# Recurrent layers: token mixes in pairs of row groups, token additions one item later

## The reference, cut to what matters

```
xa = _ln(x, ln1_w, ln1_b)
sx = jnp.concatenate([state[:, 1:2] - xa[:, :1], xa[:, :-1] - xa[:, 1:]], axis=1)
xxx = jnp.tanh((xa + sx * maa_x) @ maa_w1).reshape(b, l, 5, DM)
xxx = jnp.einsum('blfd,fde->blfe', xxx, maa_w2)
xm = xa[:, :, None] + sx[:, :, None] * (maa_stack + xxx)
xk, xw, xv, xr, xg = (xm[:, :, j] for j in range(5))
w = jnp.exp(-jnp.exp(time_decay + jnp.tanh(xw @ td_w1) @ td_w2)).reshape(b, l, h, s_)
r = (xr @ Wr.T).reshape(b, l, h, s_)
k = (xk @ Wk.T).reshape(b, l, h, s_)
v = (xv @ Wv.T).reshape(b, l, h, s_)
g = jax.nn.silu(xg @ Wg.T)
# the scan over the tokens: out = r (u * k v + s), s = k v + w * s
```

## Time and profile before

| what | value |
|---|---|
| median of 3 runs | 3045.12 us (3043.93 to 3047.5) |
| the profiled execution | 3048.42 us, its span 3046.6 us |
| mean granted clock of TensorE | 0.961 of full speed |
| TensorE (PE) busy | 2794.7 us, 92% |
| VectorE (DVE) busy | 2018.4 us, 66% |
| ScalarE (ACT) busy | 1340.0 us, 44% |
| GpSimd (POOL) busy | 665.8 us, 22% |
| one turn of the loop in L1 | 78.40 us |

### The profile page before, as it was taken

One profiled execution on the slowest core, in us unless ns is written; L12 is line 12 of the kernel. 1 busy time (PEld: TensorE's weight loads), 2 busy tenths in 40 slices (PEclk: granted clock), 3 DMA queues, 4 the chain that ended last, 5 costly groups with the idle time before them and its releaser, 6 DMA issues.

```text
span 3046.6 us, 53530 instructions
## 1 busy us (share of the span) xinstructions
PE 2794.7 (92%) x18016; PEld 2172.7 (71%) x18016; DVE 2018.4 (66%) x4920; ACT 1340.0 (44%) x3438; POOL 665.8 (22%) x436
## 2 busy tenths in 40 slices
PE   7999999878999999589999999999997889999986
PEld 7555555766888888485445554899996768888866
DVE  2778787668999999554555555411101799999992
ACT  1888888533444443353444444323220234444432
POOL 0011110034444445200000000000000444444440
PEclk9999999988999999889999999999997999999998
DMA  2101000323332333200000000300002333333340
GB/s 108 37 24 35 24 34 13 131 77 93 93 93 87 92 87 96 80 28 20 21 20 29 19 19 10 153 1 1 0 0 90 104 93 91 91 88 90 92 125 11
DMA packets 96168, 182.86 MB, mean 60 GB/s; under 512 B 10122, under 2 KB 87498, under 8 KB 92462
## 3 DMA queue, kind: packets, MB, share of 16 engines
q1 hardware_dynamic: 96046, 181.27, 19.2%
HBM read 171.34 MB, written 9.90 MB: 59 GB/s over the span
## 4 chain that ended last, share of the span: by engine, by line
PE 67%; DVE 13%; issue 10%; ACT 8%; POOL 1%; DMA 1%; DVEq 0%; SPq 0%; ACTq 0%; POOLq 0%
PE psum L519 20%; PE psum L314 10%; PE psum L1964 6%; PE psum L1851 4%; PE psum L1337 3%; DVE psum L726 3%; PE psum L510 3%; ACT arena L1617 3%; ACT arena L2231 2%; PE psum L1864 2%; PE psum L1906 2%; PE psum L526 2%; PE psum L1349 2%; DVE arena L741 2%; PE psum L533 2%
## 5 line engine op out<-in xcount | busy, mean ns | idle before, releaser
L519 PE MATMUL psum<-arena 128*128 128x200 f32 x4096 | 774.4, 348 | 51.2 <-DVE arena L902 18.6
L519 PEld LDWEIGHTS psum<-arena 128*128 128x128 f32 x4096 | 724.1, 198 | 135.7 <-issue 79.9
L1140 POOL TENSOR_TENSOR arena<-arena 128x800 f32<-128x800 f32 x256 | 454.9, 1780 | 453.8 <-DVE psum L726 453.8
L741 DVE TENSOR_TENSOR_SCAN arena<-arena,psum 128x808 f32<-128x808 f32 x256 | 469.9, 1835 | 37.2 <-PE psum L510 22.0
L314 PE MATMUL psum<-arena 128*128 128x200 f32 (+1 forms) x1920 | 332.4, 335 | 15.1 <-POOLq L139 13.4
L314 PEld LDWEIGHTS psum<-arena 128*128 128x128 f32 x1920 | 328.4, 192 | 16.9 <-POOLq L139 13.3
L1617 ACT ACTIVATE arena<-arena 100x361 f32<-100x361 f32 x512 | 300.4, 590 | 87.2 <-DVE arena L1545 85.5
L1120 POOL TENSOR_TENSOR arena<-arena 128x800 f32<-128x800 f32 x80 | 141.3, 1767 | 775.3 <-DVE arena L749 600.2
L726 DVE TENSOR_TENSOR psum<-arena 128x808 f32<-128x808 f32 x256 | 280.3, 1095 | 6.6 <-DVE arena L741 1.7
L1545 DVE CUSTOM_DVE_ANT_0 arena<-psum,arena 100x361 f32<-100x361 f32 x512 | 254.0, 530 | 45.5 <-ACT arena L1617 37.9
L1337 PEld LDWEIGHTS psum<-arena 100*128 100x128 f32 x1536 | 146.3, 142 | 131.1 <-ACT arena L1629 60.3
(11 more groups left out here) (142 smaller groups left out, 3855.1 us busy)
## 6 DMA issues: line engine op xcount, KB each, us to landing
arena<-v_rows SPq DMA_DIRECT2D x512, 202.0 KB, 3.2
arena<-ctxT SPq DMA_DIRECT2D x32, 722.0 KB, 4.3
arena<-L_w SPq DMA_DIRECT2D x9, 1024.0 KB, 10.1
arena<-L_w SPq DMA_DIRECT2D x8, 1152.0 KB, 16.0
v_rows<-arena SPq DMA_DIRECT2D x32, 202.0 KB, 2.1
arena<-L_fc SPq DMA_DIRECT2D x4, 1024.0 KB, 8.0
arena<-L_pj SPq DMA_DIRECT2D x4, 1024.0 KB, 15.8
arena<-xT SPq DMA_DIRECT2D x4, 800.0 KB, 12.2
```

What stands on the lines that cost most here:

```text
L519: mm = pe.matmul(chunk(bank, j), m.W[n][:, k, c * P:(c + 1) * P], src[:, k, :], start=k == 0, stop=k == C - 1)
L741: dve.tensor_tensor_scan(m.ring[n % 4].rearrange("p j e -> p (j e)"), m.we[:, cc].rearrange("p j e -> p (j e)"), m.kv, 0.0, ALU.mult, ALU. ...
L1140: pool.tensor_tensor(sv, sv, rb, ALU.mult).then_inc(sem("r_states"), 1)
```

## The change

The change does four things.

1. Mixes 0 and 1 become one pair, 2 and 3 another. `mix(x)` now makes two chunks of both members of its pair, x even chunks 0 and 1, x odd chunks 2 and 3. The matmuls alternate between the two members: each member has its own 32 rows of the array and its own bank (4 or 5). Mix 4 stays as it was (`last_mix`).
2. `mix_term(x)` follows: it writes two chunks of each member. xm[0] is complete only after half of mix term 1, xm[1] after the whole of it, xm[2] and xm[3] likewise in mix term 3.
3. The token additions stand at items 9 to 13 instead of 8 to 11 and 13. The place before the item's product, and behind its wait for VectorE's next product, is the same.
4. TensorE does mix 2 and the variance ahead of the k projection, and mix 3 directly behind it, ahead of the decay's first matmul.

Some waits of VectorE move with the data that they guard.

```
             def mix(x):
-                w, th, r0 = (m.w2, m.tha, DM * x) if x < 4 else (m.low, m.thl, BACK)
+                for j in range(2):
+                    for n in range(2):
+                        r0, c = DM * (x - x % 2 + n), 2 * (x % 2) + j
+                        mm = pe.matmul(chunk(4 + n, j), m.w2[r0:r0 + DM, c * P:(c + 1) * P], m.tha[r0:r0 + DM, :],
+                                       start=True, stop=True)
+                mm.then_inc(sem("mix_sum"), 1)
+
+            def last_mix():
                 for c in range(C):
-                    mm = pe.matmul(chunk(4 + c // 2, c % 2), w[r0:r0 + DM, c * P:(c + 1) * P], th[r0:r0 + DM, :],
-                                   start=True, stop=True)
+                    mm = pe.matmul(chunk(4 + c // 2, c % 2), m.low[BACK:BACK + DM, c * P:(c + 1) * P],
+                                   m.thl[BACK:BACK + DM, :], start=True, stop=True)
                 mm.then_inc(sem("mix_sum"), 1)
...
             if front:
+                wait(pe, "mix_term", f, 8)
+                mix(2)
+            if back:
+                m.n2.pe_var(pe, b)
+            if front:
                 wait(pe, "mixed", f, 1)
                 if rec and not back:
                     wait(pe, "gate", i, 2)
                 project_half("k", m.xm[0], 0, 2, "k_sum")
-                wait(pe, "mix_term", f, 8)
-                mix(2)
-            if back:
-                m.n2.pe_var(pe, b)
+                wait(pe, "mix_term", f, 12)
+                mix(3)
...
                 mm.then_inc(sem("decay_hidden_sum"), 1)
-
-                wait(pe, "mix_term", f, 12)
-                mix(3)
                 wait(pe, "mixed", f, 3)
...
                 wait(pe, "decay_rate", f, 4)
-                mix(4)
+                last_mix()
...
             def mix_term(x):
                 wait(dve, "mix_sum", f, x + 1)
-                for c in range(C):
-                    dve.scalar_tensor_tensor(m.xm[x][:, c, :], chunk(4 + c // 2, c % 2), vec(f"stack{x}", c),
-                                             m.sx[:, c, :], ALU.add, ALU.mult).then_inc(sem("mix_term"), 1)
+                for n in range(2):
+                    for j in range(2):
+                        c, y = (2 * (x % 2) + j, x - x % 2 + n) if x < 4 else (2 * n + j, x)
+                        dve.scalar_tensor_tensor(m.xm[y][:, c, :], chunk(4 + n, j), vec(f"stack{y}", c),
+                                                 m.sx[:, c, :], ALU.add, ALU.mult).then_inc(sem("mix_term"), 1)
...
             def add_token(x):
-                wait(pool, "mix_term", f, 4 * x + 4)
+                wait(pool, "mix_term", f, (6, 8, 14, 16, 20)[x])
                 pool.tensor_tensor(seq(m.xm[x]), seq(m.xm[x]), m.xs[:, :, :, 1:E], ALU.add).then_inc(sem("mixed"), 1)
...
-                if front and 8 <= n < 12:
-                    add_token(n - 8)
-                if front and n == 13:
-                    add_token(4)
+                if front and 9 <= n < 14:
+                    add_token(n - 9)
```

More of the change, by code:

```diff
@@ L852, in body @@
                     wait(dve, "k_sum", i, 2)
+                    wait(dve, "decay", i, 4)
                 mix_term(0)
@@ L865, in body @@
             if front:
-                if rec:
-                    wait(dve, "decay", i, 4)
                 mix_term(1)
@@ L874, in body @@
                     wait(dve, "v_sum", i, 2)
+                    wait(dve, "r_sum", i, 2)
+                if not rec and after.tail:
+                    dve.wait_ge(*after.done)
+                    columns()
                 mix_term(2)
@@ L884, in body @@
             if front:
[L885 to L889, removed]
                 mix_term(3)
```

## The result

The changed kernel takes 3273.28 us (median, 3271.07 to 3275.72), the kernel before 3045.49 us beside it. The ratio is 1.0739 with a 95% interval of 1.0725 to 1.0752. The change makes the kernel 7.4% slower; the forecast was 3266 us, or 7.2%.

A forecast was written before the change was run, and what follows sets the result against it. TensorE and VectorE both nearly full, the turn hanging on product 11, addition 2, v, `reduce(4)`, scan 12. 11.7 us waits plus 5.3 clock, 17 a turn: 12 x 17 + 2 x 8.6 = 221 us, forecast 3266, range 3160 to 3325.

The forecast's parts named there:

- The place that decides: Loop turn: addition 2 follows product 12, v starts at 29.5 instead of 21.95; r at 40.56 instead of 28.89.
- the clock terms of the prediction: Half clock behind new pauses, per turn: k 0.8, v 2.1, `reduce(4)` 0.2, r 2.0, mix 4 0.2; 5.3 us.
- a wait of 2.7 us ahead of the scaling: VectorE's scaling behind scan 11 could start at 21.1, but ScalarE's reciprocal deviation, made after k, is ready at 23.8.
- the walk: Predicted timeline of one loop turn, offsets from its first o projection; 11.7 us longer at full clock.
- 8.6 stood for each in the sum: First recurrent call per layer, without second norm: about 6 us of waits and 2.6 for the clock; 2 x 8.6 = 17.
- Both clock rivals: TensorE's clock stays full (3198 us, chance 0.22), or everything behind a pause is at half clock (3330, chance 0.17).
- Full clock: Rival: TensorE's clock stays full, only waits count; 152 us more, 3198 us; chance 0.22.
- Half clock for everything: Rival: everything behind a TensorE pause at half clock, 9.9 us a turn instead of 5.3; 3330 us; chance 0.17.
- The rule of strict order in start and end: Skill's rule for TensorE matmuls: five pass times left of eight in a pair, a mix saves 0.51 us, not 0.67.
- The rival that pairs don't run side by side: Mix 2 ends 0.67 us later, variance and k pushed 0.5 to 1 us a turn; about 3276 us; chance 0.08.
- The rival that the kernel gains the mixes' time: TensorE is the bound: 0.67 us saved 4 times in each of 16 fronts, 43 us, 3002 us; chance 0.03.

The follow-up runs named there:

- the filling run: Changed kernel plus matmuls that nobody reads in TensorE's three pauses, only where rec and back are there, wait for k moved ahead of the filling: 3197.88 us.
- the run with both repairs: Changed kernel with token additions ahead of GpSimd's wait for VectorE's next product, and ScalarE making the reciprocal deviation before moving k out of PSUM: 3145.19 us.
- the run that makes it true: Changed kernel with both members of a pair taken from the same 32 rows: 3304.33 us, ratio 1.0848.

## Why the prediction was right

**The place that decides.** The step that put v behind product 12, and r behind product 13, was right in kind and in size. Offsets from the start of the turn, forecast at full clock and measured with the half clock in it: mix 2 13.95 and 13.24, k 16.8 and 16.49, v 29.5 and 29.95, r 40.56 and 43.38, the feed-forward projection 45.8 and 51.26. With the clock terms of the prediction added (0.8 up to v, 3.1 up to r, 5.3 in all) the last three are 30.3, 43.7 and 51.1. In the filling run, which is at full clock, mix 2, k, v, r and the feed-forward projection start at 13.25, 16.07, 28.80, 39.71 and 44.97, all 0.7 to 0.9 us before the forecast for full clock (13.95, 16.8, 29.5, 40.56 and 45.8): one early error, and every step behind it right to 0.2 us. The run with only the additions moved shows that their place alone is enough.

**ScalarE.** Forecast was a wait of 2.7 us ahead of the scaling, measured 3.76. VectorE reached it 0.7 us earlier than in the walk (at 20.4 instead of 21.1), since a copy of 8 columns took 0.17 us instead of the 0.99 that it took before; this is the early error. Exp was done 0.4 us later than forecast, in part because k, at a lower clock, ended late (at 20.05 instead of 19.8). At full clock, in the filling run, the wait is 2.68 us. Turning the order around gave back 43 us.

**Waits and clock.** A turn was forecast at 11.7 us of waits and 5.3 of clock. By the filling run they are 10.8 and 6.3. That the sum of 17.0 holds (measured 17.1) is partly luck, since two errors cancel: the walk's waits were 0.9 too long, and the clock was taken 1.0 too low. The terms of the clock were all off by a little. The variance and k took 1.5 us more than at full clock where 0.8 stood (the variance 2.38 instead of 1.55, k 3.56 instead of 2.90, start to next start), v 2.5 where 2.1 stood and r 2.6 where 2.0 stood, while `reduce(4)` and mix 4 lost nothing where 0.2 each stood (0.81 and 1.54 us to the next start). Not all of this delays what follows, so the sum is the 6.3 of the filling run.

The first call with recurrence became 6.8 us longer in L1 and 10.9 in L3, where 8.6 stood for each in the sum. The 221 us of the whole sum are 222.7 between the two profiled executions; that the medians are 228 apart comes from which executions were profiled, 2.9 us above the median of its kernel before and 2.2 below it after.

Both clock rivals are settled. Full clock was forecast at 3198, which is what the filling run takes (3197.88), though a hit this close is chance: the run has no filling in the first calls, and its waits are 0.9 us a turn shorter than the rival's. Half clock for everything was forecast at 3330, and `reduce(4)` and mix 4, as short as at full clock, show that it doesn't hold. The Trainium skill (TensorE: Matmul & The Clock Gate, HAM oscillation) describes a kernel whose waits between bursts of matmuls are long enough that each burst begins throttled. v and r in the changed kernel agree with it (granted clock 0.52 and 0.51 behind 7.46 and 5.58 us). It doesn't follow that every new pause is paid for: v behind 3.32 us in the run with both repairs took 2.97 us.

**The pairs.** 0.88 us for a mix was forecast from rows of another layer and measured to the hundredth. The rule of strict order in start and end (the Trainium skill, TensorE: Matmul & The Clock Gate, Part 3), weighed against it, would have given 1.05 us, and 1.38 for the members one after the other. The trace disagrees with it for these matmuls: 0.88 us in both runs. The rival that pairs don't run side by side was priced at about 10 us; the run that makes it true costs 31, because mix 2 and what stands behind it fell into half clock.

**The side.** The rival that the kernel gains the mixes' time had its condition right: the third addition would have had to be done by 21.8 us of the turn, it was done at about 29.8.

## What to carry to other kernels

Where two engines are both nearly full in a loop, shortening work on one is worth nothing in front of a wait; look first which result gates the next long stretch, and follow its place through the order of every engine. When a piece moves on one engine, read the order of the engines that serve it too: here ScalarE still took k before the variance. A wait that opens can cost twice on TensorE, once as a pause and once as half clock on what follows; whether it does has to be looked up in every turn and not in one.

## What the runs showed of the hardware

- Four K=32 matmuls from two row groups into two banks took 0.88 us in both orders that were tried, 1.54 us from one row group. Eight passes in about the time of four.
- 12.6 us a turn of products that nobody reads, put into the three pauses, kept the granted clock at 1.00 through the turn, for a gain of 75 us; what they cost in power was not looked at.
- GpSimd and VectorE stretch each other when both work on SBUF: a product of 1.00 us took 2.10 to 2.40, four feed-forward mixes 2.79 instead of 1.44, the norm's scaling 2.40 instead of 0.99, and on GpSimd an addition 2.31 instead of 1.73. Scans of VectorE beside an addition kept their 1.84 us.
- The length of a pause alone doesn't tell what the clock does. In the kernel before, pauses of 1.0 to 1.2 us ahead of v were followed by half clock in four calls of a layer and by full clock in three; a pause of 3.32 us was followed by full clock in the run with both repairs.
